# Layers 2 and 3 of a four-layer network in one program per engine

## The reference, cut to what matters

```
layer 2: z = sigmoid(x) * ratio2;  per token, two experts e:  y += weight_e * down_e(silu(gate_e(z)) * up_e(z))
         x = x + z + y
layer 3: z = sigmoid(x) * SU_ug * ratio3;  t = H512(z) / sqrt(512)
         h = silu(scale_g * (W_gate t)) * (scale_u * (W_up t));  x = x + scale_o * (W_down' h)
```

## Time and profile before

| what | value |
|---|---|
| median of three runs | 1774.15 us |
| the profiled execution | 1784.06 us, span 1782.1 us |
| mean granted TensorE clock | 0.944 of 2.4 GHz |
| TensorE (PE) busy | 1542.7 us, 87% |
| VectorE (DVE) busy | 1135.3 us, 64% |
| ScalarE (ACT) busy | 987.7 us, 55% |
| GpSimd (POOL) busy | 336.4 us, 19% |
| layer 2 begins, layer 3 begins | about 834 us, about 1151 us |
| layer 3's chunks after the first | to the span's end, one batch of a chunk each 16.7 us |

### The profile page before, as it was taken

The page is one execution under the profiler, slowest core; times in us unless marked ns, Lnnn a source line. Parts: engine busy times, 40 slices in busy tenths (PEclk is TensorE's granted clock), DMA queues, the critical chain, the costliest instruction groups (busy, mean ns, idle before and its releaser), DMA issues. The chain is left out here.

```text
span 1782.1 us, 19975 instructions
## 1 busy us (share of the span) xinstructions
PE 1542.7 (87%) x6541; PEld 995.6 (56%) x6574; DVE 1135.3 (64%) x1806; ACT 987.7 (55%) x1312; POOL 336.4 (19%) x251
## 2 busy tenths in 40 slices
PE   5677587789985999997469999579999999999997
PEld 2222234444443666665434444268888888888886
DVE  7899488899996999996548787745322222222222
ACT  6765588889993999995238777534321221221210
POOL 0000011111210000000614233451231221221211
PEclk9898789999997999998779999879999999999999
DMA  7764632312202543332955454371011101001001
GB/s 282 264 218 160 226 127 84 101 64 68 70 26 67 177 148 125 108 105 102 360 186 189 137 183 144 139 275 40 1 36 36 36 1 36 36 1 36 1 20 75
DMA packets 100808, 199.82 MB, mean 112 GB/s; under 512 B 11492, under 2 KB 28388, under 8 KB 96996
## 3 DMA queue, kind: packets, MB, share of 16 engines
q1 hardware_dynamic: 95012, 180.72, 29.8%
q0 software_dynamic: 5120, 16.78, 2.6%
q10 hardware_dynamic: 576, 1.05, 0.2%
HBM read 139.79 MB, written 58.72 MB: 111 GB/s over the span
## 5 line engine op out<-in xcount | busy, mean ns | idle before, releaser
L2380 ACT ACTIVATE ffn_h<-ffn_pg,ffn_gate_chunk 128x512 f32<-128x512 f32 x64 | 44.0, 688 | 324.4 <-PE ffn_pg L2457 275.5
L2543 DVE SCALAR_TENSOR_TENSOR ffn_h<-ffn_pu,ffn_up_scale,ffn_h 128x512 f32<-128x512 f32 x64 | 48.1, 751 | 231.6 <-PE ffn_pu L2457 231.5
L2553 DVE SCALAR_TENSOR_TENSOR x<-ffn_po,ffn_out_scale,x 128x512 f32<-128x512 f32 x128 | 87.3, 745 | 149.1 <-PE ffn_po L2476 149.1
L2431 POOL TENSOR_TENSOR ffn_hl<-ffn_h,ffn_hh 128x512 fp32r<-128x512 f32 x64 | 82.5, 1289 | 413.0 <-ACT ffn_hh L2387 413.0
L961 POOL TENSOR_TENSOR l_rr<-l_rr,constants 128x1 f32<-128x1 f32 x32 | 28.9, 902 | 488.0 <-DVE l_rr L988 488.0
L2476 PE MATMUL ffn_po<-ffn_hh,ffn_wh 128*128 128x512 f32 x256 | 101.2, 395 | 3.5 <-DVE x L2553 2.9
L2457 PE MATMUL ffn_pg<-zhi,ffn_wh 128*128 128x512 f32 x256 | 101.6, 397 | 0.0
L2457 PE MATMUL ffn_pg<-zhi,ffn_wl 128*128 128x512 f32 x256 | 101.2, 395 | 0.0
L2457 PE MATMUL ffn_pu<-zhi,ffn_wh 128*128 128x512 f32 x256 | 101.1, 395 | 0.0
L2457 PE MATMUL ffn_pu<-zhi,ffn_wl 128*128 128x512 f32 x256 | 101.1, 395 | 0.0
L2457 PE MATMUL ffn_pu<-zlo,ffn_wh 128*128 128x512 f32 x256 | 101.1, 395 | 0.0
(11 more groups left out here) (348 smaller groups left out, 4082.7 us busy)
## 6 DMA issues: line engine op xcount, KB each, us to landing
wkv_k<-in_fside SPq DMA_DIRECT2D x64, 256.0 KB, 3.9
ratio<-wkv_fn SPq DMA_DIRECT2D x64, 256.0 KB, 2.3
wkv_ek<-exp_k SPq DMA_DIRECT2D x48, 256.0 KB, 3.1
wkv_ekv<-exp_k_times_v SPq DMA_DIRECT2D x48, 256.0 KB, 3.8
moe_zt<-tokens_by_slot SPq DMA_DIRECT2D x39, 256.0 KB, 2.9
expert_out<-moe_eo SPq DMA_DIRECT2D x39, 256.0 KB, 2.0
ffn_raw<-in_gated SPq DMA_DIRECT2D x8, 1024.0 KB
x<-in_x SPq DMA_DIRECT2D x4, 1024.0 KB, 7.2
```

Source lines behind the costliest of these rows:

```text
L2380: eng.activation(hf[t][:, :], p_g[t][:, :], ACT.Silu, scale=scale).then_inc(*E(f"silu{t}").inc)
L2431: eng.tensor_tensor(hl[t][slot % 2][:, :], hf[t][:, :], hh[t][slot % 2][:, :].bitcast(F32), ALU.subtract).then_inc(*E(f"hl{t}").inc)
L2543: eng.scalar_tensor_tensor(hf[t][:, :], p_u[t][:, :], scale, hf[t][:, :], ALU.mult, ALU.mult).then_inc(*E(f"h{t}").inc)
L2553: last = eng.scalar_tensor_tensor(x[:, o, :], p_o[:, o, :], out_s[:, o:o + 1], x[:, o, :], ALU.mult, ALU.add)
```

## The change

Both layers are put into one block, so each engine goes from its layer 2 program into its layer 3 program without the barrier. Where layer 3's program now touches something that layer 2's other engines may still use, an explicit wait (`over`) stands. A new class `LayerStart` holds what layer 3 needs early: it keeps a place for the first chunk's raw weights, half of the gather tiles, the gate tiles and h inside `up_front`, which is free after layer 2's last gate/up product, and it has its own small tiles for scales, diagonals and minus H. The scales are loaded at layer 2's start, behind its four constants. The first chunk's weights are loaded by SyncE's layer 2 program in turn 8, behind the store of block 35 and a wait for the last gate/up product. On VectorE the arithmetic on the scales comes after the first diagonals. The order of the first chunk is changed on TensorE, ScalarE and VectorE.

```diff
+class LayerStart:
+    def __init__(self, core, scope, d, up_front):
+        self.d, self.flat = d, up_front[:, :, :].rearrange("p k n -> p (k n)")
+        self.raw = self.flat[:, 0:WCOLS]
+        rows = [self.flat[:, WCOLS + t * CH:WCOLS + (t + 1) * CH] for t in range(TPB + CT + HT)]
+        self.parts, self.g, self.h = rows[0:TPB], rows[TPB:TPB + CT], rows[TPB + CT:]
...
+    def load_scales(self, eng):
+        for dst, name in ((self.ws[:, :, :, :].rearrange("p a b t -> p (a b t)"), "wscale_ug"), (self.out_s[:, :], "wscale_dp"),
+                          (self.su[:, :, :].rearrange("p b t -> p (b t)"), "su_dp"), (self.su_ug[:, :], "su_ug")):
+            eng.dma_start(dst, self.d[name]).then_inc(*self.in_.inc)
+    def load_weights(self, eng, i):
+        eng.dma_start(self.raw[:, 0:2 * GU], self.d["gated"][ds(i * (P // BATCH), P), :]).then_inc(*self.w_in.inc)
+        eng.dma_start(self.raw[:, 2 * GU:].rearrange("p (h n) -> p h n", h=HT),
+                      self.d["down3"][ds(i * (CHUNK // BATCH), CHUNK), :]
+                      .rearrange("(h p) n -> p h n", p=P)).then_inc(*self.w2_in[i // BATCH % 2].inc)
...
@@ experts, SyncE
                 eng.dma_start(dst, src).then_inc(*const_in.inc)
+            start.load_scales(eng)
             eng.wait_ge(*E("zero").at(0))
...
                 for n in block_of(j, 1, 0):
                     store_out(n)
+                if j == TURNS:
+                    eng.wait_ge(*E("gate_up").at(NB - 1))
+                    start.load_weights(eng, 0)
...
-            w.stored(eng)
-            for p in range(OUTS):
-                eng.wait_ge(*out_sent[p].at((NB - 1 - p) // OUTS))
...
+    def over(eng, *what):
+        for name in what:
+            if name == "results":
+                for p in range(OUTS):
+                    eng.wait_ge(*out_sent[p].at((NB - 1 - p) // OUTS))
+            elif name == "ratios":
+                w.stored(eng)
+            elif name == "sources":
+                eng.wait_ge(*E("sources").at(0))
+                for k in range(2):
+                    eng.wait_ge(*E("weight").at(k))
...
@@ gated_ffn, SyncE (its four loads of scales are gone)
+            before(eng, "results", "sources")
             for j in range(N + 6):
+                if j == 1:
+                    before(eng, "ratios")
...
@@ ScalarE
             inp.round_transformed(eng, 0)
+            silu(0, 0, 0)
+            high_h(0, 0, 0)
             inp.gate_and_round(eng, 1)
-            silu(0, 0, 0)
             silu(0, 0, 1)
-            high_h(0, 0, 0)
+            high_h(0, 0, 1)
             inp.round_transformed(eng, 1)
...
@@ TensorE
+            before(eng, "zc", "h", "hc", "eo")
             inp.cols_of_y(eng, 0)
             inp.fwht(eng, 0)
-            next_cols(1)
             product(0, 0, "gate", 0)
             product(0, 0, "up", 0)
+            next_cols(1)
             product(0, 0, "gate", 1)
+            product(0, 0, "up", 1)
             inp.fwht(eng, 1)
-            product(0, 0, "up", 1)
-            next_cols(2)
             product(1, 1, "gate", 0)
             product(1, 1, "up", 0)
+            next_cols(2)
+            product(1, 1, "gate", 1)
             eng.wait_ge(*inp.E("x").at(CT * 2 + CT - 1))
             down(0, 0)
-            product(1, 1, "gate", 1)
+            product(1, 1, "up", 1)
             eng.wait_ge(*E("x").at(0))
             inp.fwht(eng, 2)
...
@@ VectorE
             inp.constants(eng)
-            eng.wait_ge(*consts.at(2))
+            eng.wait_ge(*consts.at(3))
...
+            inp.diagonals(eng, 0)
+            before(eng, "results")
...
             chunk_scale(0, 0)
-            inp.diagonals(eng, 0)
             first_low()
             inp.gated(eng, 0)
             inp.diagonals(eng, 1)
             inp.low_transformed(eng, 0)
+            hidden(0, 0, 0)
             inp.gated(eng, 1)
             inp.diagonals(eng, 2)
-            hidden(0, 0, 0)
+            hidden(0, 0, 1)
             inp.low_transformed(eng, 1)
-            hidden(0, 0, 1)
+            hidden(1, 1, 0)
             inp.gated(eng, 2)
...
@@ build
-        with shared:
-            experts(core, c, d, of_layer(2), of_layer(3), up_front, up_in)
-        core.over("up_loaded")
-        core.over("moe_", "wkv3_", "rt_")
-        gated_ffn(core, c, d, of_layer(3))
+        with shared, nc.Block() as block:
+            start = LayerStart(core, shared, d, up_front)
+            over = experts(core, c, d, of_layer(2), of_layer(3), up_front, up_in, block, start)
+            gated_ffn(core, c, d, of_layer(3), block, over, start)
```

More of the change, by code:

```diff
@@ L1509, in __call__, with __init__ @@
         eng.wait_ge(self.event.sem, self.event.start + i * self.length + k + 1)
+class LayerStart:
[4 more added lines that the diff above has]
+        self.parts, self.g, self.h = rows[0:TPB], rows[TPB:TPB + CT], rows[TPB + CT:]
+        sb = lambda n, shape, dt=F32: core.sb(scope, n, shape, dt)
+        self.ws, self.su = sb("ffn3_ws", [P, 2, NCHUNK, HT]), sb("ffn3_su", [P, NCHUNK, HT])
+        self.out_s, self.su_ug = sb("ffn3_out_scale", [P, CT]), sb("in3_su", [P, CT])
+        self.minus_H = sb("in3_minus_H", [P, P], F32R)
+        self.diag = [[sb(f"in3_diag{k}_{t}", [P, P]) for t in range(TPB)] for k in range(2)]
+        self.in_, self.w_in, self.w2_in = core.event("ffn3_constants", 16), core.event("ffn3_weights_loaded", 16), core.dma_event("ffn3_down_loaded")
+    def load_scales(self, eng):
[7 more added lines that the diff above has]
+                      .rearrange("(h p) n -> p h n", p=P)).then_inc(*self.w2_in[i // BATCH % 2].inc)
 class LayerInput:
-    def __init__(self, core, scope, c, d, ratio, banks, spare):
+    def __init__(self, core, scope, c, d, ratio, banks, spare, start):
         self.core, self.c, self.d, self.ratio = core, c, d, ratio
@@ L1520, in __init__ @@
         self.zlo = core.sb(scope, "zlo3", [P, CT, TOK], F32R)
[L1521 removed]
+        self.g = start.g
         self.banks = banks
         self.ratio_in = [core.event(f"in3_ratio{b}", 16) for b in range(BATCH)]
[L1524 removed]
         self.e = {}
[L1526 to L1528 removed]
+        self.minus_H, self.su, self.diag = start.minus_H, start.su_ug, start.diag
+        own = [start.parts, [core.sb(scope, f"in3_part{t}", [P, CH], F32)[:, :] for t in range(TPB)]]
         lent = [[spare[k][:, t * CH:(t + 1) * CH].bitcast(F32) for t in range(TPB)] for k in range(2)]
         self.parts = [own, lent]
[L1531 removed]
         self.gathered = core.queue_event("in3_gathered", 2 * TPB)
@@ L1659, in low_transformed, with experts @@
             eng.tensor_tensor(self.low(i)[:, j, :], self.banks[:, j, :], self.high(i)[:, j, :].bitcast(F32), ALU.subtract).then_inc(*self.E("low").inc)
-def experts(core, c, d, ratio, ratio3, up_front, up_in):
+def experts(core, c, d, ratio, ratio3, up_front, up_in, block, start):
     nc = core.nc
@@ L2287, in _, with gated_ffn @@
                     w.scan_alone(eng, u, u % w.slots, "scan_n", True)
-def gated_ffn(core, c, d, ratio):
+    def over(eng, *what):
[9 more added lines that the diff above has]
+                    eng.wait_ge(*E("weight").at(k))
+            elif name in ("ratio", "newton"):
+                eng.wait_ge(*w.E(name).at(UNITS - 1))
+            else:
+                eng.wait_ge(*E(name).at(NB - 1))
+    return over
+def gated_ffn(core, c, d, ratio, block, before, start):
     nc = core.nc
@@ L2318, in gated_ffn @@
         p_o = core.banks(s, "ffn3_po", [P, CT, TIME])
-        inp = LayerInput(core, s, c, d, ratio, p_o, (wh[1], wl[1]))
-        block = s.enter_context(nc.Block())
+        inp = LayerInput(core, s, c, d, ratio, p_o, (wh[1], wl[1]), start)
         def chunk_w(parts, slot, which, k, o):
@@ L2327, in _ @@
         def _(eng):
[L2328 to L2331, removed]
             def load(i, slot):
@@ L2337, in load @@
                     eng.wait_ge(*w_lo.at(i // BATCH - 1))
[L2338 to L2341, removed]
+                start.load_weights(eng, i)
             def send_out(i, slot):
@@ L2353, in _ @@
                 for i in due(j, 0, N):
-                    load(i, i % U)
+                    if i:
+                        load(i, i % U)
                 for i in due(j, BATCH + 1, N):
@@ L2379, in silu @@
                 scale = gate_c[slot // BATCH][:, t:t + 1]
-                eng.activation(hf[t][:, :], p_g[t][:, :], ACT.Silu, scale=scale).then_inc(*E(f"silu{t}").inc)
+                eng.activation(hf[t], p_g[t][:, :], ACT.Silu, scale=scale).then_inc(*E(f"silu{t}").inc)
             def high_h(i, slot, t):
@@ L2560, in first_low @@
                 eng.tensor_tensor(wl[0][:, :], raw[:, :], wh[0][:, :].bitcast(F32), ALU.subtract).then_inc(*w_lo.inc)
+            inp.diagonals(eng, 0)
+            before(eng, "results")
+            link = Chain(core, "ffn_scales_chain", 1)
+            eng.tensor_scalar(gate_s[:, :, 0:HT], ws[:, 1, :, :], CH ** -0.5, None, ALU.mult)
```

(5 more changed lines are left out.)

54 lines of the change are left out of this document (18 added, 36 removed).

## The result

The changed kernel takes 1757.51 us (median of 4 runs, 1754.36 to 1758.13), the kernel before 1773.04 beside it: ratio 0.9904, interval [0.9885, 0.9923]. Forecast were 1760.5 and a gain of 13.7 us; it is 15.5 here, and 10.8 and 13.8 in two later sets of runs. So the total held. Not all of its terms did, and one part of the gain, about 5 us, was in none of them.

A forecast was written before the change was run, and what follows sets the result against it. The wait at the layer 2–3 seam was taken to end with the first weights' landing, gathers close behind. 11.9 + 0.7 + 3.1 − 2.0 = 13.7 us off the median 1774.15 gives 1760.5; own range 1757 to 1764, given 1754 to 1769.

The forecast's parts named there:

- both chains: Seam between layers 2 and 3: weights' landing and row gathers must both move; weights alone would gain under 1 us.
- The weights' landing: Layer 3's first weights, 1.5 MB loaded early in layer 2, should land in 6.5 to 8.5 us, by about 1142.5.
- rival (b): Early weights hold up layer 2's last stores; gathers start 3.3 us later, gain 10.4, time 1763.8; chance 0.08.
- The gathers' landing: Seam: the eighth gather, issued about 1156.9, lands 2.9 us later at 1159.8; ends 1157.3 and 1162.6.
- the gain of 11.9: Seam: first addition of expert rows to x at 1160.5 instead of 1172.44; ends 13.2 and 6.9.
- rival (a): Gathers take the weights' place: 5.75 us landing and TensorE's halt again, gain 8.7, time 1765.5; chance 0.20.
- The hold at `first_low`: Seam: VectorE's `first_low` falls across gather 7, so the eighth is out about 1156.9; without hold, 0.9 us better.
- First transform: Layer 3's first transform, 10.4 us before: TensorE's clock falls again; 0.7 gained, of 0 to 3.0 possible.
- The new order: Layer 3's first batches: 1.8 for the wait, 1.9 for the clock, −0.6 before `down`; gain 3.1, between 1.5 and 4.
- Scales in layer 2: Four small DMAs ahead of layer 2's sixteen ratio loads delay the first gating product: −2.0 us, bounds 0 and −4.
- Rival (e): Second batch: GpSimd's queue becomes the bound if the fourth batch's gathers are held; 6.6 us slower, 1780.8; chance 0.03.

The follow-up runs named there:

- before again: The kernel before, unchanged, run once more for a second profile: 1777.21 us, ratio 0.9996 to the kernel before.
- the changed kernel with padding: Changed kernel with 32 unused bytes per partition ahead of zhi and zlo, addresses going from 32 to 0 modulo 64: 1773.69 us, 0.9979 of the kernel before.
- in six pieces: Changed kernel with the 3.36 us low-parts subtraction on VectorE issued as six of 512 columns: 1756.3 us, 0.9906 of the kernel before.
- the first pair: First profiles of the kernel before and the changed kernel, nothing else altered: medians 1773.04 and 1757.51 us, ratio 0.9904.
- the old order: Changed kernel with layer 3's first-chunk order on TensorE, ScalarE and VectorE as before, the rest kept: 1760.16 us, 0.9931 of the kernel before.
- the second pair: Both kernels run again unchanged for second profiles: kernel before 1777.21 us (0.9996), changed kernel 1767.04 us (0.9936).

## Why the prediction held, and where it did not

*What bounds, and both chains.* Right: early weights with early gathers give 9 to 10 us at the seam (24.0 to 14.0; 25.9 to 16.8), the gathers early without the weights nothing. But which chain came last before the change was less settled than the prediction had it. In its one profile the weights did. In the second profile of the same kernel `first_low` ended at 1166.20, and the addition waited on for the columns (VectorE timeline, before again):

```profile
1168.66 1.29 DVE L1624 TENSOR_TENSOR x<-x,ffn_po 128x512 f32<-128x512 f32 x2 [2.46 <-PE ffn_po L1578]
```

*The weights' landing.* Right: issued from 1124.85 on, they had landed by 1132.6, 7.8 us later (forecast 6.5 to 8.5), ahead of ScalarE at 1135.48. The two stores right behind them landed late, which the prediction had left out: the one issued at 1126.99 took 6.4 us and the next 5.7, where the same two took 2.2 before. The last store, on which the gathers hang, was issued at 1132.91 and took 2.0, as before. So the first gather went out 3.3 us ahead of layer 2's end (1135.96 and 1139.25), forecast 3.4 (1145.0 and 1148.41), and rival (b) falls. The Trainium skill (DMA: Bandwidth & Descriptors, Queues, rings and completion order) has rings consumed in order, which puts stores behind the weights. The trace agrees as far as it goes: these two landed at 1133.4 or later, just behind the weights. Full DMA engines (0.85 and more from 1124 to 1132) could have delayed them as well; the runs don't separate the two.

*The gathers' landing.* This is the term that was mis-sized. I took 2.9 us because "the weights are out of the way". From the end of a pair's second issue to the matmul that waited for it, the first three pairs took 4.3 (1138.57 to 1142.87), 7.1 (1141.33 to 1148.40) and 4.9 (1145.83 to 1150.68). The gathers themselves, 256 KB each every 1.26 us, and the ratio load of 1 MB issued among them fill the DMA engines: 0.92 to 0.93 at 313 to 333 GB/s. (That load took 11.0 us, where the prediction had 6.9 at most; it was still in time for its first use.) TensorE waited 1.78 us for the second tile. So the first addition came 14.0 to 16.8 behind, not 12.1 (1160.5 − 1148.41), and the gain of 11.9 is 9 to 10. This lies between the forecast and rival (a).

*A halt that nobody priced.* Rival (a)'s halt was one of TensorE within the columns. What came in two of eleven profiles with the early gathers is another: TensorE was through with all columns, and VectorE waited on, for something that the profile doesn't name ("remote"). In the changed kernel's second profile:

```profile
1158.25 0.39 PE L1600 MATMUL ffn_po<-in_diag,in_part 128*128 128x128 f32 x2
```

```profile
1160.17 0.69 DVE L1646 TENSOR_TENSOR x<-x,ffn_po 128x512 f32<-128x512 f32 x1 [10.99 <-remote]
```

The first addition there is 1.5 us behind the columns' end instead of 1.3 ahead of it, and another 2.1 us pass between the additions (6.9 to the first transform instead of 4.8): 5 us together. That is about what this set's gain of 10.8 lacks against 15.5. The other profile is the changed kernel with padding (9.0 to the first transform). What VectorE waits for stays open.

*The hold at `first_low`.* Right that it is one gather (2.95 against 0.95), and that the row of 4.03 was no full ring. The Trainium skill (SBUF — State Buffer, Who interferes with whom) infers that tensor_tensor does not keep GpSimd from writing descriptors. The same section says that a VectorE instruction with two inputs in SBUF contends with a GpSimd instruction that reads SBUF, which the prediction did not use; `first_low` has both inputs there, and a gather takes its row numbers from there (`moe_source`). This case's runs go against the inference and agree with the second sentence: each time the held gather ends 0.8 us behind the instruction's end (1145.83 and 1145.02 after; 1173.26 and 1172.44 before), and in six pieces the hold is gone. Whether it is the reading that is held, no run shows. Wrong that the hold costs time: without it the third tile was there no sooner (1150.77 against 1150.68).

*First transform.* Forecast 0.7 gained; 10.4 to 10.3 in the first pair, 9.3 to 9.4 in the second: nothing. The clock was 0.52 again after 3.5 us of idle:

```profile
1158.00:1164.00 6.00, 6.00 (x15) 4.75 (x16) 4.72 (x13) 1.82 (x3) 4.54 (x5) 0.52 0.86 283
```

*The new order.* Forecast 3.1, measured 1.9 in the first pair, 1.3 to 1.7 against the old order, and nothing in the second pair, where the kernel before had its clock up in the same columns (7.41 instead of 9.04, in its chain) and the changed one waited 0.5 for the low halves behind its second transform. So the 1.9 for the clock is there in some executions only; the wait of 1.82 goes. What I left out: the first product behind a transform now takes 3.00 instead of 2.75 and starts 0.1 late, three times up to the fourth transform, 1.1 together; why, the runs don't show. The wait ahead of `down` is 0.66, and comes twice, as forecast (0.6).

```profile
1210.68 0.50 PE L2506 MATMUL ffn_po<-ffn_hh,ffn_wh 128*128 128x512 f32 x1 [0.66 <-DVE x L1646]
```

*Scales in layer 2.* Forecast −2.0; 2.0 at the first product, 2.6 at the end of layer 2, 3.1 in the time.

*Rival (e).* The fourth batch's gathers took 1.45 and then 0.95: none was held. Beside other VectorE work no gather took over 1.56 us in any profile of the changed kernel.

*The sum.* In the first pair 10.0 + 0.1 + 1.9 − 2.0 is 10.0 us, at the lower edge of the forecast's own range (10 to 17 us); with the 5.1 of the buffers' place it is 15.1, beside 15.5 measured. The time was met because an unforeseen gain stood in for what the landing and the order did not bring. Nothing in the trace of before could show it; the diff could, since it moves buffers, but I did not look at addresses. Take 5 us off in each set, and what the forecast had priced brought 10.5, 6 and 9 us instead of 13.7: the direction was right, the size of the total came out by luck.

## What to carry to other kernels

When a wait is moved forward together with the transfers behind it, price the new landing by the bytes that will be in flight then, not by the quietest landing of the old trace. Loads put ahead of a stage's first inputs cost their full issue time there if the whole stage hangs on these; put them behind the last load of that stage. When a change moves buffers, compare a steady loop that it doesn't touch before giving the whole difference to the edit.

## What the runs showed of the hardware

- A product of 12 matmuls took 2.80 us with `zhi` and `zlo` at 0 over a multiple of 64 bytes and the weights at 32, and 2.75 with both at 32; 32 unused bytes moved the kernel by 7.3 and 6.7 us of 1770, in opposite directions, of which 5.6 and 5.9 are in the stretch of these products. Which of the two sides' reading it slows was not tried.
- A subtraction of 128x3072 with both operands in SBUF (3.36 us) stretched one indirect DMA's issue to 2.95 to 4.03 us instead of 0.95, in all twelve profiles that have it; six of 128x512 (3.82 together) stretched none.
- Gathers of 256 KB beside a load of 1 MB landed 4.3 to 7.1 us after their issue, and one issued 1.9 us sooner did not land sooner.
- With 1.5 MB of loads issued just ahead, two stores of 256 KB took 6.4 and 5.7 us to land instead of 2.2.
- After the same wait of 2.9 us the last 24 matmuls took 5.74 us in three profiles and 7.05 to 7.35 in eleven.
